# A decoder layer on one core: five places for probabilities in cross attention, outputs taken a pair later, VectorE's side work spread; experts with one table of results and adding scatters

## The chip, the cores and the metric

The kernel runs on one core of a Trainium2 chip. The metric is the device time of one launch in microseconds (us), as the median of several runs. The core has five engines with queues of their own: TensorE (PE) multiplies matrices into PSUM, VectorE (DVE) and ScalarE (ACT) work on PSUM and SBUF, GpSimd (POOL) works on SBUF, and SyncE (SP) issues transfers (DMAs). They meet only at semaphores. PEld is TensorE's loading of weights.

## The reference: what is computed

One decoder layer with post-normalisation, in f32, over 8 batches of 512 rows of 256. Three stages follow each other, each adding to its input and normalising the sum:

- self attention (16 heads of 64, across the batch of 8, for each of the 512 positions);
- cross attention of the 512 rows of each batch with 1024 context rows: both are normalised with a gain and bias, keys are rotated with cos and sin, the scores are clipped to -11 and 11 before the softmax, and the heads' outputs go through Wo;
- a mixture of 8 experts (hidden size 512, SiLU gate) with the best 2 for each of 4096 tokens, plus one shared expert for all.

```
attn = jnp.clip(jnp.einsum('bhnd,bhsd->bhns', q, k) * scale, -11.0, 11.0)
out = jnp.einsum('bhns,bhsd->bhnd', jax.nn.softmax(attn, axis=-1), v) @ Wo + bo
...
h = jnp.einsum('bsd,edh->bseh', x, W1) * jax.nn.silu(jnp.einsum('bsd,edh->bseh', x, W3))
out = sum over the two experts of (h @ W2) * w + shared expert
x = layernorm(x + out)
```

Products that need more than the matmul's own precision are made in three terms, from a high part (an f32r copy by ScalarE) and a low part (what the copy left out, a subtraction on VectorE or GpSimd).

## The kernel before

**Cross attention** (`cross_attention`) loops over 8 batches. A batch has two halves (g) of 8 heads; a half first makes keys and values in 8 tiles (`keys_values`, L881; the keys are rotated on VectorE and turned by TensorE, L917), and then goes through 4 pairs (p) of heads. A pair has 4 steps (j) of two units (a); a unit is 128 context rows by 2 heads by 512 queries, so 128x1024 values.

The work of one unit passes five engines' queues: TensorE makes the scores (L837, L845) into one of two pairs of PSUM banks; ScalarE takes the exponential into SBUF (L1071); GpSimd clips it there (L816, the clip of the scores done on their exponentials); TensorE multiplies the clipped unit with the values (L958); VectorE adds it to the pair's running sum `acc` (L1218, L1221). The exponentials have four places in `probs`, two for each parity of the step (`at_step`), so one of step j waits for `pv_done` and `acc_ready` of step j-2.

TensorE's order is written out: scores of the next step, in step 0 also the sums of the last pair (L865, a matmul of `acc` with ones) and the queries of the next (L857), then the products with the values. In the second half a step of each pair also transposes context rows for the next batch (L890).

What each pair leaves is worked up during the next: `inverse` takes the reciprocal of the sums in four quarters (L1194), `o_scaled` multiplies (L1201) into the single tile `o`, `o_hi` copies its high part on ScalarE (L1005), and `o_lo` the low one on VectorE (L1205); the project with Wo (L972) comes at the half's end. All of this stands in VectorE's queue between the accumulations, with the low part of the next queries (`q_lo`, L1173), and for the next batch the statistics of its rows (L1101, first half), their normalising (L1112) and the low part of the turned context (`context_lo`, L1116; second half). ScalarE has `o_hi` of pair p-1 at the end of step 3 of pair p, ahead of pair p+1's first exponentials. GpSimd has one power of a small tile for that normalising (L820), behind the second half's first two clips.

**Experts** (`experts`): 4096 tokens go in 16 dense units of 256 through the shared expert, and then sorted by expert in 39 units. Routing makes a place for each token and expert; 64 indirect DMAs scatter the rows into the sorted table `xs`. For each unit TensorE runs `first` (W3, W1; L1664) and `second` (W2; L1682), and between the halves of `first` it turns the rows of the next unit (`turn`, L1645). SP loads rows (`load_rows`, L1475) and weights (`load_w`, L1462) in one queue, in order; ScalarE and GpSimd and VectorE split the weights into high and low parts. GpSimd splits the next set's weights and then sends a unit's results (`send`, L1559): two indirect DMAs of 128 rows to the table `ys` in DRAM.

A token's two results go to two halves of `ys` (`SECOND` apart), so that no row is written twice; `goals` works out which. The dense results stay in SBUF (`take`, L1890) and eight additions join them with the input (`add_dense`, L1906), one in each of eight units from the third expert unit on. At the end both halves of `ys` are loaded in chunks of 512 tokens (L1504, L1771), GpSimd adds the two (`both`, L1574), VectorE adds the sum to the rest and takes the statistics (`combine`), GpSimd takes the power (`root`), ScalarE normalises (L1775), and SP stores.

## Time and profile before

| what | us |
|---|---|
| median of 3 runs (lowest, highest) | 3220.79 (3215.07, 3221.74) |
| profiled execution | 3219.01 |
| its span, first to last instruction | 3217.3 |
| mean granted TensorE clock | 0.965 |
| busy: PE, PEld | 2890.4 (90%), 1966.5 (61%) |
| busy: DVE, ACT, POOL | 2210.6 (69%), 1433.4 (45%), 1470.0 (46%) |

Cross attention lies from about 660 to 2610 us of the span and the experts from there to the end. Batch 3 (the fourth) of cross attention, from which most rows below are, goes from 1404.5 to 1642.5. A window's granted clock is a share of full speed: 1.00 is 2.4 GHz, and a stretch at 0.50 is 1.2 GHz. In the timelines a line is a run of like instructions: start, duration, engine, line, operation, output and inputs, count, and in brackets how long the engine was idle before it and what ended that.

### The profile page before, as it was taken

How to read it: one execution, taken by the hardware profiler on the slowest of the kernel's cores; microseconds unless marked ns; L12 is line 12 of the kernel's file. 1: busy time of each engine (PE TensorE's matmuls, PEld its weight loads, DVE VectorE, ACT ScalarE, POOL GpSimd, SP SyncE). 2: the span in 40 equal slices, each digit the busy share in tenths (PEclk: the TensorE clock that was granted, in tenths of full speed). 3: DMA queues.
4: the chain of work that ended last, by engine and by line, in shares of the span. 5: the costliest groups of instructions: out<-in, count | busy, mean ns of one | idle time of the engine just before them, and what ended most of it. 6: DMA issues, size and time to landing. Idle time of an engine off the chain costs nothing. (4 is left out here: it accounts for less than half of the span.)

```text
span 3217.3 us, 52631 instructions
## 1 busy us (share of the span) xinstructions
PE 2890.4 (90%) x17208; PEld 1966.5 (61%) x17256; DVE 2210.6 (69%) x3538; ACT 1433.4 (45%) x2076; POOL 1470.0 (46%) x1060
## 2 busy tenths in 40 slices
PE   6999999969999999999999999999899879999993
PEld 4888888844554454454454454454454449999992
DVE  3555555557768777678767777767767774598886
ACT  2222222253554553554554554554554532455553
POOL 1222222225445545545545545545545525466666
PEclk9999999989999999999999999999999989999996
DMA  9000000020010010010010010010010023266665
GB/s 255 14 15 14 15 14 15 14 66 8 14 39 10 14 41 7 14 41 7 14 41 7 14 41 7 14 41 7 14 41 7 14 79 117 101 210 222 225 223 192
DMA packets 137039, 180.91 MB, mean 56 GB/s; under 512 B 16992, under 2 KB 96864, under 8 KB 136736
## 3 DMA queue, kind: packets, MB, share of 16 engines
q1 hardware_dynamic: 115696, 143.74, 14.7%
q10 hardware_dynamic: 14224, 14.58, 1.7%
q0 software_dynamic: 6816, 18.75, 1.7%
q8 instruction: 166, 2.72, 0.4%
q14 instruction: 137, 1.12, 0.1%
HBM read 118.54 MB, written 41.71 MB: 50 GB/s over the span
## 5 line engine op out<-in xcount | busy, mean ns | idle before, releaser
L816 POOL TENSOR_SCALAR raw<-raw 128x1024 f32<-128x1024 f32 x512 | 737.7, 1441 | 452.8 <-ACT raw L1071 431.6
L1071 ACT ACTIVATE raw<-b_ps 128x1024 f32<-128x1024 f32 x512 | 498.7, 1020 | 398.3 <-PE b_ps L845 299.0
L1221 DVE TENSOR_TENSOR b_acc<-b_acc,raw 128x1024 f32<-128x1024 f32 x384 | 507.9, 1323 | 133.9 <-POOL raw L816 118.5
L958 PE MATMUL b_ps<-raw 128*64 128x512 f32 x2048 | 513.5, 617 | 43.4 <-POOL raw L816 43.0
L837 PE MATMUL b_ps<-b_QQ,b_KT 128*128 128x512 f32 x1024 | 334.9, 437 | 96.9 <-ACT raw L1071 92.6
L837 PEld LDWEIGHTS b_ps<-b_QQ,b_KT 128*128 128x128 f32 x1024 | 168.4, 191 | 336.4 <-ACT raw L1071 191.7
L802 POOL TENSOR_TENSOR b_QQ<-raw,b_QQ 128x512 fp32r<-128x512 f32 x128 | 165.5, 1293 | 390.6 <-ACT b_QQ L1025 390.6
L1664 PE MATMUL c_ps<-c_xT_l,c_w_h 128*128 128x256 f32 x1504 | 306.0, 287 | 8.6 <-DVE c_xT_l L1934 4.2
L958 PEld LDWEIGHTS b_ps<-raw 128*64 128x64 f32 x2048 | 121.3, 138 | 314.2 <-POOL raw L816 160.0
L1664 PEld LDWEIGHTS c_ps<-c_xT_l,c_w_h 128*128 128x128 f32 x1504 | 243.3, 192 | 14.4 <-issue 14.0
L1194 DVE RECIPROCAL b_r<-b_ps 128x128 f32<-128x128 f32 x256 | 234.6, 937 | 15.2 <-PE b_ps L865 13.7
L1542 POOL TENSOR_TENSOR c_w_l<-c_raw,c_w_h 128x1024 fp32r<-128x1024 f32 x80 | 169.5, 2138 | 151.0 <-ACT c_w_h L1715 151.0
L273 POOL TENSOR_TENSOR a_Pe<-a_Sc,a_same 128x2048 f32<-128x2048 f32 x32 | 117.7, 3679 | 234.8 <-DVE a_Sc L517 161.6
L1218 DVE TENSOR_TENSOR b_acc<-raw 128x1024 f32<-128x1024 f32 x64 | 85.3, 1333 | 196.5 <-POOL raw L816 196.5
L845 PE MATMUL b_ps<-b_QQ,b_KT 64*128 64x512 f32 x1024 | 194.7, 459 | 0.0
L501 DVE TENSOR_REDUCE a_Sc<-a_ps 128x32 f32<-128x512 f32 x128 | 80.9, 684 | 149.8 <-PE a_ps L331 149.8
L1664 PE MATMUL c_ps<-c_xT_l,c_w_l 128*128 128x256 f32 x624 | 176.4, 283 | 0.0
L1738 ACT ACTIVATE c_hT_h<-c_hid 128x512 fp32r<-128x512 f32 x110 | 69.5, 632 | 209.3 <-DVE c_hid L1913 209.3
L1045 ACT ACTIVATE b_KT<-b_ps 128x512 fp32r<-128x512 f32 x256 | 138.7, 598 | 33.0 <-PE b_ps L917 33.0
L1124 DVE TENSOR_TENSOR raw<-b_ps,b_cos 128x512 f32<-128x512 f32 x129 | 88.8, 689 | 90.5 <-PE b_ps L881 85.7
L1005 ACT ACTIVATE b_OT_h<-b_o 128x512 fp32r<-128x512 f32 x64 | 40.4, 631 | 225.0 <-DVE b_o L1201 225.0
L1025 ACT ACTIVATE b_QQ<-raw 128x512 fp32r<-128x512 f32 x129 | 81.6, 632 | 130.2 <-DVE raw L1136 129.9
(261 smaller groups left out, 6784.4 us busy)
## 6 DMA issues: line engine op xcount, KB each, us to landing
c_raw<-in_L_ffn_W_dram SPq DMA_DIRECT2D x117, 512.0 KB, 4.4
b_QQ<-b_QQ SPq DMA_DIRECT2D x128, 128.0 KB, 2.4
xs<-zeros ACTq DMA_DIRECT2D x1, 10140.0 KB, 66.6
c_xg<-xs SPq DMA_DIRECT2D x39, 260.0 KB, 5.8
b_rows<-in_ctx_dram SPq DMA_DIRECT2D x9, 1024.0 KB, 7.4
a_xt<-in_x_dram SPq DMA_DIRECT2D x72, 64.0 KB, 2.2
b_rows<-x SPq DMA_DIRECT2D x9, 512.0 KB, 7.0
x<-a_x1t SPq DMA_DIRECT2D x64, 64.0 KB, 1.9
```

The costliest lines, as they stand in the source:

```text
L273: pool.tensor_tensor(Pe[:, :, :].rearrange("p h (t b) -> p (h t) b", b=BI), Sc[:, t % 2].rearrange("p h t -> p (h t)").unsqueeze(2).broadc ...
L802: pool.tensor_tensor(nat[:, :, 1:3, :], krot[:, t % 2, :].rearrange("p (q a n) -> p q a n", a=2, n=HD), nat[:, :, 0::3, :].bitcast(F32), A ...
L816: pool.tensor_scalar(pr, pr, HI, LO, ALU.min, ALU.max).then_inc(clipped, 1)
L837: pe.matmul(bank(key, hh), KT[:, 2 * p + hh, t * P:(t + 1) * P], QQ[:, n % 2, hh, 0, :], start=True, stop=False)
L845: mm = pe.matmul(bank(key, hh), KT[own, 2 * p + hh, t * P:(t + 1) * P], QQ[own, n % 2, hh, 1, :], start=False, stop=True)
L958: mm = pe.matmul(bank(key)[hh * HD:(hh + 1) * HD, :], V[:, t, (2 * p + hh) * HD:(2 * p + hh + 1) * HD], probs[:, at_step(j, a), hh * B:(hh ...
L1045: drain(key, act.activation(KT[:, 4 * a:4 * a + 4, t * P:(t + 1) * P], bank(key).rearrange("p (h n) -> p h n", n=P), ACT.Copy))
L1071: ins = act.activation(probs[:, at_step(j, a), :], both(key), ACT.Exp, scale=SCALE)
L1194: ins = dve.reciprocal(r[:, a * P:(a + 1) * P], bank(key)[:, a * P:(a + 1) * P])
L1221: dve.tensor_tensor(total, total, pr, ALU.add).then_inc(acc_ready, 1)
L1542: pool.tensor_tensor(WS[m][n % 2][1][:, cols], raw[:, n % 2, m, cols], WS[m][n % 2][0][:, cols].bitcast(F32), ALU.subtract).then_inc(w_rea ...
L1664: mm = pe.matmul(ps[:, 2 * s + m, (hb % 2) * T:(hb % 2 + 1) * T], lhsT, rhs, start=(a == 0), stop=(a == 3 * KD - 1))
```

## The change

Cross attention:
- The exponentials have five places, the four of `probs` and a tile `fifth`, taken in turn by units counted through the half. An exponential waits for `pv_done` and `acc_ready` of the unit five before it; `pv_done` counts units instead of steps. The query tile `QQ` is split into `QH` and a smaller `QL`, and `knat` lies over a part of `QH` and `fifth`.
- ScalarE takes `o_hi` of pair p-2 at step 2 of pair p (the last but one behind the loop).
- VectorE's side work is ordered anew: `inverse` has one quarter at (1,0), (2,0), (2,1) and (3,0) each, `o_lo` moves to (3,0), `o_scaled` to (3,1), the row statistics to (0,0), the normalising of four row tiles is cut into two and two, and `context_lo` goes to (1,0). GpSimd's power of the second half comes behind step 1's clips.

Experts:
- `ys` has one row for each token (and spare ones). The dense result is added to the input as it is taken out of PSUM, SP stores it into `ys` (`store_dense`), and each send adds to `ys` (`compute_op`). A send waits until the one before has landed, the first until all dense results have.
- Seven of the eight dense stores stand in SP's queue ahead of the first `load_rows`, the eighth behind the second.
- `add_dense`, `both` and the additions in `combine` go. At the end each chunk is loaded once, by SP and ScalarE in turn.

```diff
+        def unit(p, j, a):
+            return (p * 4 + j) * 2 + a
+        def place(u):
+            n = (u + 2) % 5
+            return probs[:, n, :] if n < 4 else fifth[:, :]
...
-                                if (g, p, j) == (1, 0, 0):
+                                if (g, p, j) == (1, 0, 1):
                                     pool.wait_ge(var_ready, 2 * b + 2)
                                     pool.tensor_tensor(rs[:, :], ve[:, :], mhalf[:, :], ALU.pow).then_inc(rstd_ready, 1)
...
-                                mm.then_inc(pv_done, 1)
+                                    mm.then_inc(pv_done, 1)
...
-                                    if (p, j) >= (0, 2):
-                                        before = step(g, p, j) - 2
-                                        act.wait_ge(pv_done, b * (8 * PG) + before + 1)
-                                        act.wait_ge(acc_ready, b * (16 * PG) + before * 2 + a + 1)
-                                    ins = act.activation(probs[:, at_step(j, a), :], both(key), ACT.Exp, scale=SCALE)
+                                    u = unit(p, j, a)
+                                    if u >= 5:
+                                        act.wait_ge(pv_done, b * (16 * PG) + g * (8 * PG) + u - 4)
+                                        act.wait_ge(acc_ready, b * (16 * PG) + g * (8 * PG) + u - 4)
+                                    ins = act.activation(place(unit(p, j, a)), both(key), ACT.Exp, scale=SCALE)
...
-                                if j == 3 and p:
-                                    o_hi(b, g, p - 1)
+                                if j == 2 and p >= 2:
+                                    o_hi(b, g, p - 2)
+                        o_hi(b, g, PG - 2)
...
-                                    if 0 < p < PG - 1 and at == (3, 0):
-                                        o_scaled(p - 1)
-                                    if p:
-                                        quarters = {(1, 0): (0,), (2, 0): (1,), (2, 1): (2, 3)}
-                                        if p == PG - 1:
-                                            quarters = {(1, 0): (0,), (1, 1): (1,), (2, 0): (2,), (2, 1): (3,)}
-                                        for quarter in quarters.get(at, ()):
-                                            inverse(p - 1, quarter)
                                     if p + 1 < PG and at == (1, 1):
                                         q_lo(p + 1)
-                                    if p >= 2 and at == (0, 0):
+                                    if p and at in ((1, 0), (2, 0), (2, 1), (3, 0)):
+                                        inverse(p - 1, ((1, 0), (2, 0), (2, 1), (3, 0)).index(at))
+                                    if p >= 2 and at == (3, 0):
                                         o_lo(p - 2)
+                                    if 0 < p < PG - 1 and at == (3, 1):
+                                        o_scaled(p - 1)
...
+                def store_dense(c):
+                    sp.wait_ge(y_drained, 2 * c + 2)
+                    sp.dma_start(totals(c), dense[c]).then_inc(totals_in, 16)
...
+                for c in range(CH - 1):
+                    store_dense(c)
                 sp.wait_ge(scattered, 16 * 2 * NT)
                 load_rows(0)
                 load_rows(1)
+                store_dense(CH - 1)
...
                 def send(j):
                     pool.wait_ge(y_drained, DENSE + j + 1)
+                    if j:
+                        pool.wait_ge(sent[(j - 1) % 2], 16 * TT * ((j - 1) // 2 + 1))
+                    else:
+                        pool.wait_ge(totals_in, 16 * CH)
                     for t in range(TT):
                         pool.indirect_dma_start(
...
-                            in_=yr[:, j % 2, t, :], in_offset=None).then_inc(sent[j % 2], 16)
+                            in_=yr[:, j % 2, t, :], in_offset=None, compute_op=ALU.add).then_inc(sent[j % 2], 16)
...
-                        ins = dve.tensor_copy(dense[u // 2][:, 2 * (u % 2):2 * (u % 2) + 2, :].rearrange("p t d -> p (t d)"), src)
+                        ins = dve.tensor_tensor(dense[u // 2][:, 2 * (u % 2):2 * (u % 2) + 2, :],
+                                                src.rearrange("p (t d) -> p t d", d=D),
+                                                y[:, 2 * u:2 * u + 2, 0:D], ALU.add)
...
-                    if DENSE + 2 <= u < DENSE + 2 + CH:
-                        add_dense(u - DENSE - 2)
...
-                    dve.wait_ge(pooled, c + 1)
-                    dve.wait_ge(dense_added, c + 1)
-                    at = y[:, c * CT:(c + 1) * CT, 0:D]
-                    chained(dve.tensor_tensor(at, at, dense[c], ALU.add))
+                    dve.wait_ge(x_in[c], 32)
```

## Rows read from the trace of the kernel before

**Rows 1.** TensorE's waits in batch 3: waiter, releaser, us, times, longest
```profile
PE b_ps L837 <- ACT raw L1071: 11.8, 13, 2.7
PE b_ps L958 <- POOL raw L816: 5.4, 6, 1.1
```

**Rows 2.** Windows at batch 3's sums: length; busy PE, PEld, DVE, ACT, POOL; clock
```profile
1433.20:1456.30 23.10, 22.20 (x104) 9.79 (x103) 15.35 (x15) 14.59 (x21) 18.51 (x13) 1.00 0.05 13
1456.30:1475.90 19.60, 17.64 (x76) 6.93 (x76) 15.59 (x18) 9.20 (x11) 12.78 (x9) 1.00 0.06 14
...
1495.50:1510.20 14.70, 12.27 (x54) 3.98 (x53) 13.17 (x15) 5.82 (x6) 9.74 (x7) 1.00 0.01 2
1545.00:1570.80 25.80, 23.12 (x110) 10.38 (x110) 16.01 (x29) 15.75 (x22) 17.61 (x13) 1.00 0.05 11
1570.80:1594.10 23.30, 19.05 (x80) 7.66 (x82) 18.73 (x21) 10.95 (x14) 11.84 (x9) 0.95 0.05 12
1594.10:1615.60 21.50, 18.78 (x80) 7.38 (x80) 16.89 (x21) 10.58 (x13) 10.56 (x8) 0.97 0.06 13
1615.60:1632.70 17.10, 14.79 (x59) 4.81 (x57) 12.72 (x13) 7.11 (x8) 8.67 (x6) 0.90 0.00 0
```

**Rows 3.** TensorE's timeline: pair 1 of the first half, pair 0 of the second
```profile
1456.30 1.08 PE L865 MATMUL b_ps<-b_acc,b_ones 128*64 128x512 f32 x4 [0.28 <-DVE b_acc L1221]
...
1458.89 1.94 PE L958 MATMUL b_ps<-raw 128*64 128x512 f32 x8
...
1469.93 1.94 PE L958 MATMUL b_ps<-raw 128*64 128x512 f32 x8
...
1566.19 0.66 PE L890 MATMUL b_ps<-ident,b_rows 128*128 128x128 f32 x4 [0.64 <-DVE b_rows L1112]
```

**Rows 4.** ScalarE's timeline at the end of pair 1 of the first half
```profile
1472.05 0.63 ACT L1005 ACTIVATE b_OT_h<-b_o 128x512 fp32r<-128x512 f32 x1 [3.81 <-DVE b_o L1201]
```

**Rows 5.** GpSimd's and VectorE's timelines, then two lines' durations in ns: min/median/max
```profile
1473.78 2.17 POOL L816 TENSOR_SCALAR raw<-raw 128x1024 f32<-128x1024 f32 x2 [3.44 <-ACT raw L1071]
...
1505.24 3.55 POOL L816 TENSOR_SCALAR raw<-raw 128x1024 f32<-128x1024 f32 x2 [0.77 <-ACT raw L1071]
...
1506.67 1.22 DVE L1221 TENSOR_TENSOR b_acc<-b_acc,raw 128x1024 f32<-128x1024 f32 x1
...
L1221 DVE TENSOR_TENSOR b_acc<-b_acc,raw x384: 1153/1225/2056, 722.5 to 2588.3; 128x1024 f32<-128x1024 f32 x192
...
L1112 DVE TENSOR_SCALAR b_rows<-b_rows,b_mv,b_rs x108: 395/406/1207, 672.9 to 2553.5; 128x256 f32<-128x256 f32 x108
```

**Rows 6.** Timelines of SP, VectorE, TensorE at the first expert units; loads' landing (us)
```profile
2765.16 0.82 SPq L1475 DMA_DIRECT2D c_xg<-xs  x2
...
2780.04 0.69 DVE L1890 COPY c_dense<-c_ps 128x512 f32<-128x512 f32 x1 [0.74 <-PE c_ps L1682]
...
2798.40 0.68 DVE L1890 COPY c_dense<-c_ps 128x512 f32<-128x512 f32 x1
...
2782.72 0.60 PE L1645 MATMUL c_ps<-ident,c_xg 128*128 128x128 f32 x4
...
2800.86 0.60 PE L1645 MATMUL c_ps<-ident,c_xg 128*128 128x128 f32 x4
...
c_xg<-xs SPq DMA_DIRECT2D x39, 260.0 KB, 5.8
```

**Rows 7.** Windows: an expert unit with `add_dense`, one without; columns as above
```profile
2817.30:2827.40 10.10, 10.10 (x87) 10.10 (x86) 9.19 (x20) 5.64 (x9) 6.74 (x4) 1.00 0.60 211
...
2907.40:2916.80 9.40, 9.27 (x78) 9.09 (x77) 8.07 (x18) 5.51 (x9) 6.08 (x4) 1.00 0.67 224
```

**Rows 8.** Scatters' landing (us); windows: last chunk's statistics, final loads to the end
```profile
c_ys<-c_yr,c_goal_u POOLq DMA_INDIRECT x78, 2.4
...
3206.50:3209.90 3.40, 0.00 (x0) 0.00 (x0) 3.25 (x12) 2.08 (x5) 2.06 (x2) 0.50 0.14 47
3167.90:3217.30 49.40, 0.00 (x0) 0.00 (x0) 32.91 (x88) 16.48 (x32) 33.77 (x16) 0.50 0.78 255
```

More of the change, by code:

```diff
@@ L812, in _ @@
                                 for a in range(2):
-                                    pr = probs[:, at_step(j, a), :]
+                                    pr = place(unit(p, j, a))
                                     wait_drained(pool, ("s", g, p, j, a), b)
@@ L959, in _ @@
                                                        V[:, t, (2 * p + hh) * HD:(2 * p + hh + 1) * HD],
-                                                       probs[:, at_step(j, a), hh * B:(hh + 1) * B],
+                                                       place(unit(p, j, a))[:, hh * B:(hh + 1) * B],
                                                        start=(t == 0), stop=(t == CT - 1))
-                                mm.then_inc(pv_done, 1)
+                                    mm.then_inc(pv_done, 1)
                         def project(a, pairs):
@@ L999, in q_hi @@
                         own = slice(hh * HD, (hh + 1) * HD)
-                        ins = act.activation(QQ[own, n % 2, hh, 0, :], bank(key)[own, :], ACT.Copy)
+                        ins = act.activation(QH[own, n % 2, hh, :], bank(key)[own, :], ACT.Copy)
                     ins.then_inc(qh_ready, 1)
@@ L1172, in q_lo @@
                                 own = slice(hh * HD, (hh + 1) * HD)
-                                ins = dve.tensor_tensor(QQ[own, n % 2, hh, 1, :], bank(key)[own, :],
-                                                        QQ[own, n % 2, hh, 0, :].bitcast(F32), ALU.subtract)
+                                ins = dve.tensor_tensor(QL[own, n % 2, :], bank(key)[own, :],
+                                                        QH[own, n % 2, hh, :].bitcast(F32), ALU.subtract)
                             ins.then_inc(q_ready, 1)
@@ L1212, in _ @@
                                     at = (j, a)
-                                    pr = probs[:, at_step(j, a), :]
+                                    pr = place(unit(p, j, a))
                                     total = acc[:, p % 2].rearrange("p h n -> p (h n)")
@@ L1217, in _ @@
                                     if at == (0, 1):
-                                        dve.tensor_tensor(total, probs[:, at_step(0, 0), :], pr, ALU.add).then_inc(acc_ready, 2)
+                                        dve.tensor_tensor(total, place(unit(p, 0, 0)), pr, ALU.add).then_inc(acc_ready, 2)
                                     elif j:
@@ L1242, in _ @@
                                         variances(b, FIRST + b * TAKEN + ROWS)
-                                    if g == 1 and p < 3 and at == (((2, 0), (0, 1), (0, 1))[p]):
-                                        if p == 0:
-                                            dve.wait_ge(rstd_ready, 2 * b + 2)
-                                        for t in range(4 * p, 4 * p + 4):
-                                            normalise(t, rows[:, t, :], rows[:, t, :], normed)
-                                    if g == 1 and p and at == (0, 1):
+                                    if g == 1 and p < 3:
+                                        halves = ((2, 0), (2, 1)) if p == 0 else ((0, 0), (0, 1))
+                                        if at in halves:
+                                            if (p, at) == (0, (2, 0)):
+                                                dve.wait_ge(rstd_ready, 2 * b + 2)
+                                            t0 = 4 * p + 2 * halves.index(at)
+                                            for t in (t0, t0 + 1):
+                                                normalise(t, rows[:, t, :], rows[:, t, :], normed)
+                                    if g == 1 and p and at == (1, 0):
                                         context_lo(p - 1)
@@ L1337, in experts @@
         dense = [over("dense", c, 0) for c in range(CH)]
-        other = [raw[:, 0, c, :].rearrange("p (t d) -> p t d", d=D) if c < 2 else over("other", c, 1) for c in range(CH)]
         wr = sb("c_wr", [P, KD, E])
@@ L1447, in logit_bank, with totals @@
             return ps[:, 7 - 2 * (c % 2), (c // 2) * CT * E:(c // 2 + 1) * CT * E]
-        def results(half, c):
-            return ys[half * SECOND + 1 + c * 512:half * SECOND + 1 + (c + 1) * 512].rearrange("(t p) d -> p t d", p=P)
+        def totals(c):
+            return ys[1 + c * 512:1 + (c + 1) * 512].rearrange("(t p) d -> p t d", p=P)
         with nc.Block() as block:
@@ L1501, in _ @@
                     sp.wait_ge(sent[k], 16 * TT * ((TILES + 1 - k) // 2))
-                for c in range(CH):
-                    sp.wait_ge(dense_added, c + 1)
-                    sp.dma_start(dense[c], results(0, c)).then_inc(x_in[c], 16)
+                for c in range(0, CH, 2):
+                    sp.dma_start(y[:, c * CT:(c + 1) * CT, 0:D], totals(c)).then_inc(x_in[c], 16)
                 for c in range(CH):
@@ L1570, in _ @@
                 send(TILES - 1)
-                def both(c):
-                    pool.wait_ge(x_in[c], 48)
-                    pool.tensor_tensor(dense[c], dense[c], other[c], ALU.add).then_inc(pooled, 1)
                 def root(c):
@@ L1582, in _ @@
                 for c in range(CH):
-                    both(c)
-                    if c:
-                        root(c - 1)
-                root(CH - 1)
+                    root(c)
             @block.tensor
@@ L1767, in _ @@
                     act.wait_ge(sent[k], 16 * TT * ((TILES + 1 - k) // 2))
-                for m in range(2):
-                    wait_split(act, SETS - 1, m)
-                for c in range(CH):
-                    act.dma_start(other[c], results(1, c)).then_inc(x_in[c], 16)
+                for c in range(1, CH, 2):
+                    act.dma_start(y[:, c * CT:(c + 1) * CT, 0:D], totals(c)).then_inc(x_in[c], 16)
                 for c in range(CH):
@@ L1899, in take @@
                     ins.then_inc(y_drained, 1)
-                def add_dense(c):
-                    dve.wait_ge(scattered, 16 * 2 * NT)
-                    dve.wait_ge(y_drained, 2 * c + 2)
-                    at = y[:, c * CT:(c + 1) * CT, 0:D]
-                    dve.tensor_tensor(at, at, dense[c], ALU.add).then_inc(dense_added, 1)
                 def product(u, s):
```

43 lines of the change are left out of this document (18 added, 25 removed).

## The prediction

> **What bounds the kernel now.** I read the busy table first, then the waits of TensorE over one batch of cross attention, then windows cut at the pairs, and last each engine's timeline around a pair's end. The chain that ended last reaches back only through the experts, so it says nothing of the 1950 us of cross attention. There TensorE waits in one batch 11.8 us for exponentials and 5.4 us for clipped probabilities [rows 1]. The windows show where: the same pair of heads takes 19.6 us in a first half but 23.3 and 21.5 us in a second, and the four of a first half end with one of 14.7 us [rows 2]. Without a gap a pair with queries needs 2.59 us for sums and queries and four steps of (1469.93 - 1458.89) / 3 = 3.68 us, together 17.3 us [rows 3]. What is above that is one stall at the pair's end: ScalarE stands 3.81 us before the o_hi copy, waiting for o_scaled on VectorE, with the next pair's exponentials queued behind it [rows 4].
>
> There is a second limit close by. A clip on GpSimd takes 1.08 us when VectorE is quiet (2.17 for two), but two clips took 3.55 us when an accumulation ran at 1506.67: the first ended when that began, the second started when it had ended; the two operations' shortest are 1.15 us for the accumulation and 0.40 for a normalise of one row tile [rows 5]. So clips and accumulations go one after the other. Eight clips and seven accumulations are 8 x 1.08 + 7 x 1.15 = 16.7 us of a pair.
>
> The Trainium skill, page "SBUF — State Buffer", section "SBUF: two separate sides", calls the port pair of VectorE and GpSimd an exclusive lock held for a whole instruction, by a VectorE operation with two SBUF inputs too. By it clips and accumulations add up as I add them; were the port shared in proportion, TensorE alone would set the pairs, which is rival A.
>
> **The change part by part.** The sums are made against the profiled execution (3219.0 us, span 3217.3), which is 1.8 us under the median of the runs.
>
> *Output copies a pair later, five places, spread side work.* The o_hi copy of pair p-2 stands at step 2 of pair p, where o_scaled is a pair old, so ScalarE no longer waits 3.81 us. An exponential waits for the unit five back, not for a whole step two back; that slack is about one unit, 1.8 us of TensorE. It costs no instruction. What is late next is the port, pair by pair:
> - First half, pair 1: TensorE 17.3, port 16.7; both near full, so I add 0.4: 17.7 against 19.6, gain 1.9. Pair 2 has an o_lo on the port as well (half the accumulation's size, about 0.6): gain 1.8. Pair 3 was at the port already (six clips and seven accumulations are 14.5 of its 14.7 us) and now gets an o_lo that stood in its first unit: loss 0.4. Pair 0 stays. Sum 3.3.
> - Second half, pair 0: 25.8 against 23.1 in the first half, of which the four added transposes are 0.6 [rows 2, 3]. The power on GpSimd goes behind the second unit's clips: of the 2.1 left I take 1.5. Below nothing it is bounded by the later normalise, two rows after (2,1): about 1.2 lost if the transposes wait for it. Pair 1: port 16.7 + four normalises of 0.41 [rows 5] + context_lo 0.6 = 18.9, with 0.5 of imperfect packing 19.4 against 23.3: 3.9. Pair 2, with o_lo, 20.0 against 21.5: 1.5. Pair 3: loss 0.3. Sum 6.6.
> - Clock: a last pair at granted clock 0.90 took 17.1 us, the first half's 14.7 at 1.00; 0.6 of the difference is transposes, 1.8 is clock [rows 2]. In this batch three pairs of the second half have a reduced clock, each behind such a stall [rows 2]; with shorter ones I take back two thirds of that loss a batch, 1.2.
>
> Per batch 3.3 + 6.6 + 1.2 = 11.1, for eight batches 89 us. The bounds: nothing gained in pairs 1 and 2 of the second half and half elsewhere, 4 a batch (32 us); TensorE alone as limit, 14.5 a batch (116 us), with all clock back 20 (160 us). The 14.5 are the two waits' 17.2 [rows 1] less 2.7 that I leave at the half's ends and behind the context's high part.
>
> *pv_done by unit, QL/QH split:* the same matmuls and copies, operands elsewhere; the place of five overlaps the key tile whose transposes ScalarE has read before unit 2. Nothing.
>
> *Experts, dense results.* The copy out of PSUM becomes an addition of the same size, 0.69 us either way (nothing). Eight additions on VectorE go: their units take 10.1 us, later ones 9.4 [rows 7]: 8 x 0.7 = 5.6 gained. One small operation of the goals goes, off TensorE's path: nothing.
>
> *The stores in SP's queue.* Seven stores now stand ahead of the first row loads, which were issued at 2765.16. The seventh waits for the dense result of unit 13, taken at 2780.04 + 0.69 = 2780.7. Two issues are 0.8 and the load lands 5.8 after its issue: 2787.4, where the transposes wanted it at 2782.72: 4.7 us of idle TensorE [rows 6]. The eighth store waits for unit 15, taken at 2798.40 + 0.68 + 4.7 = 2803.8; behind it queue the weight loads of set 3 and the next rows (four issues, 1.7, then 5.8): 2811.3, where the transposes at 2800.86 + 4.7 = 2805.6 wanted them: 5.7. Later sets are asked for early enough. With 2.5 us of reduced clock after each (the last pair above lost 1.8 so) this costs 15.5; bounds 5 (loads landing at half that) and 28 (the weights' second wave late too).
>
> *Adding scatters.* A plain scatter lands in 2.4 us, a load of rows in 5.8 [rows 6, 8]. No row shows an adding one: between 2.4 and 5.8 + 2.4 = 8.2. I take 4, since it is the same 128 rows on the same queue as the 2.4. Each send now waits for the one before; that was issued a unit (9.4 us) earlier, so GpSimd, whose next weight split is queued behind, waits for nothing. At the end the last two sends follow closely: 2 x (4 - 2.4) + 0.4 = 3.6 lost (0.4 to 12).
>
> The Trainium skill, page "DMA: Bandwidth & Descriptors", section "Rules for kernel authors", says an accumulating DMA reads its destination and writes it later. By it the add costs the read as well; with a row load's time for the read the end would lose 12 instead of 3.6, and the sum come to 3133.
>
> *The end.* From the loads' issue to the end are 49.4 us, paced by a sum on GpSimd and one on VectorE for each of eight chunks. Now 5.8 for the first load, eight chunks of VectorE's 3.25 - 1.2 (the sum of that size) plus waits = 2.2 each, and about 6 of the 7.4 us from the last statistic (3209.9) to the end [rows 8]: 29.4. Gain 20, less 3.6.
>
> Experts together: 5.6 + 20 - 3.6 - 15.5 = 6.5.
>
> **Sum:** 3219.0 - 89 - 6.5 = 3123.5, with the median's 1.8 about 3125 us; its own range is 3100 to 3150.
>
> **The rivals.**
> A. The port packs better than I add (GpSimd and VectorE merely slow each other) and TensorE bounds the pairs: 14.5 to 20 a batch, 27 to 71 us more than the forecast: 3098 to 3054, say 3090. For it: TensorE's waits on these two engines are 17.2 a batch [rows 1]. Against: the 3.55 us.
> B. The stall moves. VectorE is busy 18.73 us of the second half's pair 1 [rows 2], against the 17.3 + 0.6 that TensorE needs; its lag shows up at the sums and at the fifth place, and half is gained: 5 a batch, 40 in all, with the experts' 6.5: 3221 - 46 = 3175. Against it: pairs 0 and 3 give VectorE time to catch up.
> C. The adding scatter is slow. A send takes X us from its first issue to its last landing, and the next waits for that; above the unit's 9.4 us it holds GpSimd, behind it the next set's weight split, and so TensorE, 37 times. With 8.2 for a landing and about 1 for the second issue X is 9.2: nothing in the units and 8 at the end, 3133. It decides against the change from X = 11.7: 37 x 2.3 = 85 and 12 at the end. At 13 it is 133 + 15: about 3273. Against it: the 2.4 us of the plain scatter.
> D. It doesn't do what it says: exponentials still end on the same accumulation, and cross attention keeps its time: 3214.
>
> **How the numbers follow.** Forecast 0.58, A 0.18, B 0.14, C from 11.7 up 0.05 (below that it is within the forecast's range), D 0.05. The range 3075 to 3175 leaves out half of A, some of B, C and D. A difference within 0.2% (6.4 us) can't be told from none; D is half in it. Faster 0.92, same 0.03, slower 0.05.
>
> **What would show it.** Right: no o_hi wait on ScalarE in a pair; first-half pairs 1 and 2 at 17.5 to 18, second-half ones at 19 to 20.5; clips lengthened by accumulations and TensorE's remaining gaps ending on a clip; two idle stretches of about 5 us at the first experts' units; units of 9.4 throughout; some 30 us after the last scatter. Wrong: pairs still over 21 in second halves (B), below 18.2 (A), expert units above 9.6 (C).

## The result, and the profile after

Beside the kernel before on the same chip (3220.11 us median of 4 runs), the changed kernel took 3127.37 us (4 runs, 3115.70 to 3130.13): ratio 0.971, 95% interval 0.968 to 0.974. A second set of runs gave 3120.69 against 3225.01, 0.969 (0.966 to 0.973). The forecast was 3125 us, its own range 3100 to 3150 and that with the rivals 3075 to 3175; the measured time lies in both, 2 us from the forecast.

The profiled execution (3130.13 us, span 3128.4) splits as follows, beside a second profiled execution of the same kernel (span 3110.5, below called the repeat). Cross attention runs from its first scores to the experts' first matmul, the units from the first expert tile's transposes to the last's:

| us | before | after | repeat |
|---|---|---|---|
| up to cross attention | 711.1 | 708.3 | 711.8 |
| cross attention | 1902.7 | 1817.6 | 1802.9 |
| dense part of the experts | 169.0 | 172.1 | 170.2 |
| 38 expert units | 359.9 | 368.4 | 364.6 |
| from there to the end | 74.6 | 62.0 | 61.0 |

So cross attention gave nearly all of it: 85 us in this profile, 100 in the repeat. The experts gave 1 us in this one (603.5 to 602.5) and 8 in the repeat.

The windows of a batch at the sums (length; busy PE, PEld, DVE, ACT, POOL; granted clock; DMA), four pairs of the first half, then four of the second, here of batch 2:

```profile
1162.10:1185.10 23.00, 22.11 (x105) 10.01 (x104) 16.30 (x16) 14.70 (x21) 18.69 (x13) 1.00 0.05 13
1185.10:1202.90 17.80, 17.37 (x74) 6.90 (x74) 15.76 (x20) 8.63 (x10) 14.44 (x9) 1.00 0.07 16
1202.90:1220.80 17.90, 17.47 (x76) 6.91 (x74) 15.06 (x16) 9.46 (x11) 13.55 (x9) 1.00 0.06 15
1220.80:1236.70 15.90, 13.30 (x54) 3.90 (x52) 13.83 (x17) 6.34 (x7) 12.80 (x7) 0.95 0.01 2
1272.40:1298.90 26.50, 23.03 (x111) 10.33 (x109) 17.82 (x32) 15.80 (x22) 19.67 (x13) 1.00 0.05 11
1298.90:1317.20 18.30, 18.12 (x80) 7.23 (x78) 17.16 (x19) 10.32 (x12) 13.29 (x8) 1.00 0.07 16
1317.20:1335.40 18.20, 18.03 (x80) 7.42 (x78) 17.86 (x19) 10.77 (x13) 9.59 (x8) 1.00 0.07 15
1335.40:1351.20 15.80, 13.17 (x58) 4.45 (x57) 13.40 (x15) 7.69 (x9) 10.70 (x7) 1.00 0.00 0
```

Against [rows 2] pairs 1 and 2 fell from 19.6 to 17.9 in the first half and from 23.3 and 21.5 to 18.3 and 18.2 in the second. In all four TensorE's busy time is now within 0.5 us of the window. Pair 0 of the second half went the other way, from 25.8 to 26.5.

TensorE's waits over that batch (waiter, releaser, us, times, longest), and ScalarE at the place of [rows 4], in batch 3:

```profile
PE b_ps L967 <- POOL raw L825: 7.2, 9, 1.1
...
PE b_ps L846 <- ACT raw L1080: 1.1, 6, 0.2
...
PE b_ps L899 <- DVE b_rows L1122: 0.9, 1, 0.9
```

```profile
1441.34 0.63 ACT L1014 ACTIVATE b_OT_h<-b_o 128x512 fp32r<-128x512 f32 x1
```

The wait for exponentials went from 11.8 us a batch [rows 1] to 1.1 (and 0.2 for those in the fifth place), and the o_hi copy waits for nothing there (the next, behind the half's last exponential, still waits 6.12 us for o_scaled). What grew is the wait for clips, 5.4 to 7.2. The timelines of GpSimd, TensorE and VectorE at the end of a first half show where it sits:

```profile
1458.77 6.39 POOL L825 TENSOR_SCALAR raw<-raw 128x1024 f32<-128x1024 f32 x3
...
1460.90 1.08 PE L967 MATMUL b_ps<-raw 128*64 128x512 f32 x4 [0.44 <-POOL raw L825]
...
1463.04 1.23 DVE L1231 TENSOR_TENSOR b_acc<-b_acc,raw 128x1024 f32<-128x1024 f32 x1
...
1463.06 1.08 PE L967 MATMUL b_ps<-raw 128*64 128x512 f32 x4 [1.08 <-POOL raw L825]
...
1465.22 1.08 PE L967 MATMUL b_ps<-raw 128*64 128x512 f32 x4 [1.08 <-POOL raw L825]
...
1466.99 1.68 PE L874 MATMUL b_ps<-b_acc,b_ones 128*64 128x512 f32 x4 [0.69 <-DVE b_acc L1231]
```

Three clips take 6.39 us, 2.13 each, where one alone takes 1.08 [rows 5]; an accumulation of 1.2 us stands between one and the next. With no other work left TensorE follows at that pitch.

In the experts, the landing of the scatters (median us), GpSimd's waits over the units, and some links of the chain of waits:

```profile
c_ys<-c_yr,c_goal_u POOLq DMA_INDIRECT x78, 4.5
```

```profile
POOL c_ys L1574 <- DMA c_ys<-c_yr,c_goal_u: 59.9, 29, 3.7
```

```profile
2799.59 1.56 POOL c_ys L1574
...
2801.46 8.83 DMA c_ys<-c_yr,c_goal_u
...
2811.02 1.56 POOL c_ys L1574
...
2812.89 6.92 DMA c_ys<-c_yr,c_goal_u
...
2820.55 1.58 POOL c_ys L1574
```

A send's first issue follows that of the send before by 9.5 to 11.4 us here: the first issue, 1.87 with what follows it, then 6.9 to 8.8 from the start of the second issue to its landing, then the next send. But for the second and third, which the second stall below and a reduced clock behind it lengthen to 14.7 and 11.4 us, the units of TensorE are 9.06 to 9.13 us up to the fifteenth; from the next on, at 9.2 to 11.5, the sends set them, as a run below tests. TensorE's first two late tiles, answering [rows 6], and the window from the final loads to the end, answering [rows 8]:

```profile
2697.96 0.66 PE L1653 MATMUL c_ps<-ident,c_xg 128*128 128x128 f32 x4 [2.30 <-DMA c_xg<-xs]
...
2721.82 1.11 PE L1653 MATMUL c_ps<-ident,c_xg 128*128 128x128 f32 x4 [5.51 <-DMA c_xg<-xs]
```

```profile
3099.57:3128.40 28.83, 0.00 (x0) 0.00 (x0) 15.64 (x80) 16.06 (x32) 8.10 (x8) 0.50 0.87 291
```

### The profile page after: what moved, and what is told of

It reads as the page before. It is cut to its first block and busy times, and to the rows that moved or that the text cites. A ratio compares the mean times of both kernels' runs of the same rounds, so it can differ in the third digit from the quotient of the medians.

```text
span 3128.4 us, 52086 instructions
## 1 busy us (share of the span) xinstructions
PE 2871.6 (92%) x17208; PEld 1966.8 (63%) x17256; DVE 2198.0 (70%) x3444; ACT 1435.1 (46%) x2076; POOL 1581.4 (51%) x1051
## 5 line engine op out<-in xcount | busy, mean ns | idle before, releaser
L1080 ACT ACTIVATE raw<-b_ps 128x1024 f32<-128x1024 f32 x416 | 410.7, 1021 | 366.6 <-PE b_ps L854 318.6
L967 PE MATMUL b_ps<-raw 128*64 128x512 f32 x1664 | 423.7, 612 | 57.2 <-POOL raw L825 57.2
L1231 DVE TENSOR_TENSOR b_acc<-b_acc,raw 128x1024 f32<-128x1024 f32 x304 | 399.3, 1313 | 89.9 <-POOL raw L825 80.3
L811 POOL TENSOR_TENSOR b_knat<-raw,b_knat 128x512 fp32r<-128x512 f32 x128 | 165.4, 1292 | 404.2 <-ACT b_knat L1034 404.2
L846 PE MATMUL b_ps<-b_QH,b_KT 128*128 128x512 f32 x1024 | 325.2, 430 | 14.8 <-ACT raw L1080 9.1
L846 PEld LDWEIGHTS b_ps<-b_QH,b_KT 128*128 128x128 f32 x1024 | 168.8, 189 | 245.1 <-issue 157.4
L854 PE MATMUL b_ps<-b_QL,b_KT 64*128 64x512 f32 x1024 | 188.1, 445 | 0.0
L825 POOL TENSOR_SCALAR b_fifth<-b_fifth 128x1024 f32<-128x1024 f32 x96 | 137.1, 1428 | 81.3 <-ACT b_fifth L1080 76.8
L1574 POOL DMA_INDIRECT c_ys<-c_yr,c_goal_u x78 | 127.8, 1639 | 75.2 <-DMA c_ys<-c_yr,c_goal_u 59.9
L1820 DVE TENSOR_TENSOR c_w_l<-c_raw,c_w_h 128x1024 fp32r<-128x1024 f32 (+1 forms) x80 | 128.6, 1607 | 22.9 <-ACT c_w_h L1723 22.9
```

What stands on the lines that cost most here:

```text
L811: pool.tensor_tensor(nat[:, :, 1:3, :], krot[:, t % 2, :].rearrange("p (q a n) -> p q a n", a=2, n=HD), nat[:, :, 0::3, :].bitcast(F32), A ...
L825: pool.tensor_scalar(pr, pr, HI, LO, ALU.min, ALU.max).then_inc(clipped, 1)
L846: pe.matmul(bank(key, hh), KT[:, 2 * p + hh, t * P:(t + 1) * P], QH[:, n % 2, hh, :], start=True, stop=False)
L854: mm = pe.matmul(bank(key, hh), KT[own, 2 * p + hh, t * P:(t + 1) * P], QL[own, n % 2, :], start=False, stop=True)
L967: mm = pe.matmul(bank(key)[hh * HD:(hh + 1) * HD, :], V[:, t, (2 * p + hh) * HD:(2 * p + hh + 1) * HD], place(unit(p, j, a))[:, hh * B:(hh ...
L1080: ins = act.activation(place(unit(p, j, a)), both(key), ACT.Exp, scale=SCALE)
```

## The experiments

**Each half of the change alone.** Two kernels: the changed cross attention with the experts of before, and the reverse.

> The changed cross attention with the experts of before. Theory (the parts add up: in the two profiles cross attention gives 85 us and the experts 1): 3135 us (3130 to 3140), with the first expert units at 9.4 to 10.1 us as before. Rival (the experts pay or gain by what cross attention leaves, a clock or a filled queue): outside 3130 to 3140.

> The changed experts with the cross attention of before. Theory (what the end gives, 20 us, and the units and stalls cost, 19 us, nearly cancel): 3219 us, no difference from before within 0.2%. Rival (the gain that the prediction worked out, 6.5 us, is there and the profiles hid it): 3213 us or less.

Cross attention alone: 3117.70 us against 3224.25, ratio 0.967 (0.965 to 0.969), outside the expected band on the fast side. Experts alone: 3220.36, ratio 0.998 (0.9965 to 1.000), as the theory had it; their parts are 172.4, 369.9 and 61.3, together 603.6 us against 603.5. So the experts' edits cancel, within an interval that reaches down to 3213 us, and the gain is cross attention's. Its size was misjudged from one profile: here cross attention took 1803.4 us, 14 less than in the profile after, though the pairs have the same lengths but for three. The next run says why.

**The changed kernel again.** No edit.

> The changed kernel itself, once more, beside the three below. Of four profiles with its cross attention that part took 1818, 1803, 1802 and 1808 us with 69, 30, 26 and 42 us of it at half clock. Theory (the pairs are always the same, the reduced clock is not, and the first profile had much of it): 1800 to 1818 us for cross attention with no pair changed, 3110 to 3130 in all. Rival (the experts' part of the change slows cross attention): 1815 us or more for cross attention, 3125 us or more.

3120.69 us (0.969, 0.966 to 0.973). The windows over all of cross attention, after and repeat (columns as above):

```profile
708.30:2525.80 1817.50, 1702.26 (x8112) 919.54 (x8110) 1413.98 (x1802) 934.47 (x1284) 1036.93 (x674) 0.98 0.08 21
```

```profile
711.80:2514.70 1802.90, 1685.85 (x8112) 910.32 (x8111) 1416.77 (x1802) 934.18 (x1284) 1037.23 (x674) 0.99 0.08 21
```

The repeat's pairs agree with those of the profile after to 0.03 us, but for three second-half pairs 0 that had a reduced clock there (27.3 instead of 26.5). Most of the rest of the difference lies between the halves, from a half's last sums to the next half's first scores: 39.7 us (to the next batch) and 35.7 (within a batch) on average after, 39.1 and 34.9 in the repeat. Summed over cross attention, TensorE had 110 us at half clock before, 69 after and 30 in the repeat. The theory holds: the profile after was a long one by its clock. The pairs, 166.2 us a batch before (both halves) and 153.4 in the repeat, give 12.8 us a batch.

**Four places instead of five.**

```
-            n = (u + 2) % 5
+            n = (u + 2) % 4
...
-                                    if u >= 5:
-                                        act.wait_ge(pv_done, ... + u - 4)
-                                        act.wait_ge(acc_ready, ... + u - 4)
+                                    if u >= 4:
+                                        act.wait_ge(pv_done, ... + u - 3)
+                                        act.wait_ge(acc_ready, ... + u - 3)
```

> The changed kernel with four places for probabilities, so that an exponential waits for the unit four back. Theory (the later output copies took the stall away; four units of TensorE are some 8.9 us, which is longer than one exponential, clip and accumulation after another): pairs 1 and 2 at most 0.5 us longer, 3125 to 3135 us. Rival (the fifth place is what lets the exponentials run on): pairs 1 and 2 at 19.5 to 21.5 us, 3155 us or more.

3122.65 us, ratio 0.967 (0.964 to 0.969). Pair 1 of a first and of a second half:

```profile
1647.50:1665.40 17.90, 17.47 (x76) 6.91 (x76) 15.82 (x20) 8.62 (x11) 14.54 (x9) 1.00 0.07 16
...
1760.40:1778.70 18.30, 18.13 (x80) 7.23 (x78) 17.16 (x19) 10.33 (x12) 13.29 (x8) 1.00 0.07 16
```

No pair is longer. With the outputs taken later, the fifth place buys nothing that can be measured. The time is a little under the expected band.

**Outputs where they were.** Five places and the spread side work stay.

```
-                                if j == 2 and p >= 2:
-                                    o_hi(b, g, p - 2)
-                        o_hi(b, g, PG - 2)
+                                if j == 3 and p:
+                                    o_hi(b, g, p - 1)
```

On VectorE o_scaled, inverse and o_lo stand at the units of before as well.

> The changed kernel with the outputs taken where they were before: the scaling behind unit (3,0) of the next pair, the high copy at that pair's end, the low copy in the first unit of the pair after it. The five places and the spread side work stay. Theory (the stall of ScalarE at the high copy, 3.8 us, is back, less about one unit of 1.8 us that the fifth place gives): pairs 1 and 2 at 19 to 20.5 us, 3155 to 3185 us in all. Rival (five places alone were enough): pairs within 0.5 us of the changed kernel, 3125 to 3135 us.

3193.51 us, ratio 0.991 (0.989 to 0.993), a little above the expected band. ScalarE at the end of a first half's pair 1, and the windows of pairs 1 and 2 of both halves:

```profile
1697.75 0.63 ACT L1014 ACTIVATE b_OT_h<-b_o 128x512 fp32r<-128x512 f32 x1 [3.81 <-DVE b_o L1210]
```

```profile
1682.10:1701.60 19.50, 17.54 (x76) 6.89 (x76) 16.44 (x21) 9.10 (x11) 12.77 (x9) 1.00 0.06 14
1701.60:1721.10 19.50, 17.54 (x76) 6.90 (x74) 15.60 (x18) 9.46 (x11) 11.04 (x9) 1.00 0.06 13
1797.00:1818.00 21.00, 18.22 (x82) 7.36 (x80) 17.87 (x21) 10.86 (x14) 11.37 (x8) 1.00 0.06 14
1818.00:1841.40 23.40, 20.70 (x82) 8.38 (x82) 17.36 (x19) 10.95 (x14) 11.20 (x8) 0.86 0.05 12
```

The stall is back with the same 3.81 us as in [rows 4], the first-half pairs are 19.5 us, nearly the 19.6 of before, and cross attention is 1884 us, 81 above the repeat. Five places did not take the stall away; taking the outputs later did. (Moving only some of an output's steps was not tried; the quarters of `inverse` went back with them.) These 81 us are not all of the 100: cross attention is still some 18 us under that of before here (1902.7), most of it in the pairs, 164.3 us a batch against 166.2. So the five places, the side work or both give that much where the outputs are early. Beside late outputs each of the two can go without loss, the one in the run above, the other in the run below; taking away both at once was not tried.

**Side work where it was.** Statistics and normalises unsplit behind unit (0,1), the power behind (0,0).

```
-                                if (g, p, j) == (1, 0, 1):
+                                if (g, p, j) == (1, 0, 0):
...
-                                        halves = ((2, 0), (2, 1)) if p == 0 else ((0, 0), (0, 1))
+                                    if g == 1 and p < 3 and at == (((2, 0), (0, 1), (0, 1))[p]):
```

> The changed kernel with VectorE's side work where it was before: statistics and the context's normalises in one piece behind unit (0,1), the context's low part there too, and the power on GpSimd behind unit (0,0). Theory (it is the later power and the two halves of normalises that made pair 0 of the second half longer, 26.5 us against 25.8; in the other pairs the same work stands at the same port): pair 0 of the second half 25 to 26, pair 1 at 18.3 to 19, 3120 to 3130 us. Rival (the spreading is part of the gain): second halves 2 us longer or more, 3145 us or more.

3122.20 us, ratio 0.967 (0.966 to 0.969). Pair 0 of a first half, pairs 0 and 1 of a second:

```profile
1622.20:1645.90 23.70, 22.20 (x105) 9.99 (x104) 15.95 (x15) 14.70 (x21) 19.46 (x13) 1.00 0.05 12
...
1731.80:1757.50 25.70, 23.05 (x109) 10.33 (x107) 16.08 (x29) 15.81 (x22) 17.63 (x13) 1.00 0.05 11
1757.50:1775.90 18.40, 18.13 (x80) 7.35 (x79) 17.09 (x19) 10.31 (x12) 13.45 (x9) 1.00 0.07 16
```

The 0.7 us of the second half's pair 0 come back (25.7), the first half's pair 0 loses as much (23.7 against 23.0), and the pairs 3 cancel: the first half's is 0.5 shorter, the second's 0.5 longer. Pairs 1 and 2 don't care where four normalises stand. Over a batch it is 153.4 us either way: beside late outputs, spreading the statistics, the normalises and `context_lo` and moving the power gave nothing.

**Clips of half the size.** One line: `half = pr[:, 0:B]` is clipped instead of `pr`.

> The changed kernel with clips of half the size; left out is the clipping of every second head's probabilities. A clip falls from 1.08 us to some 0.6 and the work of the port that GpSimd and VectorE share by 4 us a pair. Theory (since the change TensorE sets pairs 1 and 2, the port only the end of a half): pairs 1 and 2 lose no more than their one gap of 0.43 us (17.4 to 17.9 in first halves, 17.9 to 18.3 in second), pair 3 falls by 1 us or more, 3080 to 3105 us. Rival (the port still sets the pairs): pairs 1 and 2 fall by 0.8 us or more.

3061.09 us, ratio 0.950 (0.947 to 0.953). Pairs 1 and 3 of a first half, then 0, 1, 2 of a second:

```profile
1617.80:1635.10 17.30, 17.30 (x78) 7.14 (x77) 14.12 (x18) 8.96 (x11) 7.45 (x8) 1.00 0.07 16
...
1652.30:1666.50 14.20, 12.26 (x56) 4.11 (x55) 13.17 (x17) 6.33 (x7) 7.42 (x6) 1.00 0.01 2
1701.20:1725.30 24.10, 23.05 (x111) 10.33 (x109) 16.06 (x32) 15.68 (x23) 14.47 (x13) 1.00 0.05 12
1725.30:1743.60 18.30, 18.06 (x82) 7.39 (x80) 15.76 (x20) 10.31 (x12) 7.46 (x8) 1.00 0.07 16
1743.60:1761.80 18.20, 18.03 (x80) 7.40 (x78) 16.01 (x19) 10.76 (x13) 6.93 (x8) 1.00 0.07 15
```

In second halves GpSimd's busy time falls from 13.3 and 9.6 us to 7.5 and 6.9, and the pairs 1 and 2 stay at 18.3 and 18.2: there TensorE sets them, and the port (what VectorE and GpSimd share) does not. In first halves they lose 0.66 us, between the two expectations, a part of the clips' pace that TensorE still waited for. Where GpSimd or the port does bind is pair 0 of the second half (26.5 to 24.1) and the ends of the halves (15.9 to 14.2, and 15.7 to 15.0). This run can't tell the two apart, since a half clip is also shorter in itself; the last run, which takes an accumulation of VectorE's out there, can.

**Scatters that write instead of adding.** One argument: `compute_op=ALU.add` goes.

> The changed kernel with scatters that write instead of adding; left out is the addition of the two experts' results and of the dense result. Theory (an adding scatter takes so long from its issue to its landing that the next one waits on GpSimd, the weight split behind it comes late, and so TensorE): the units after the sixteenth fall from 9.2 to 11.5 us to about 9.06 throughout, 16 us in all, a landing is 2.4 to 3 us, the last two sends are about 4 us shorter: 3107 us (3102 to 3112). Rival (those units are long because the weight loads or the rows arrive late, whatever the scatter does): units as before this edit, only the last sends shorter: 3123 us.

3094.53 us, ratio 0.961 (0.959 to 0.962), below the expected band: cross attention took 1801.9 us in its profile, 16 less than in the profile after. Its experts are 580.2 us against 602.5. Landings, and GpSimd's instructions over the units (count, busy us, mean ns, idle before), first of the plain kernel, then of the one after:

```profile
c_ys<-c_yr,c_goal_u POOLq DMA_INDIRECT x78, 2.4
...
L1574 POOL DMA_INDIRECT c_ys<-c_yr,c_goal_u x50 | 48.8, 975 | 11.5 <-issue 11.4
```

```profile
L1574 POOL DMA_INDIRECT c_ys<-c_yr,c_goal_u x54 | 86.4, 1600 | 57.2 <-DMA c_ys<-c_yr,c_goal_u 48.0 <-issue 9.2
```

Behind the two stalls the units are 9.06 us up to the 28th and at most 9.23 then, 353.0 in all, 15.4 less; from there to the end it is 54.9 instead of 62.0. The theory holds: adding costs 22.5 us against the profile after (15.4 and 7.1), 17.7 against the repeat (11.6 and 6.1).

**The goals' two small operations back, on top of the plain scatters.**

```
+                    dve.scalar_tensor_tensor(goal[:, 0, :], eid, own, nought[:, :], ALU.not_equal, ALU.mult)
...
-                    dve.tensor_tensor(goal_u[:, q, :], token, goal[:, 1, :], ALU.add)
+                    link(dve.tensor_tensor(goal[:, 3, :], goal[:, 0, :], token, ALU.add))
+                    dve.tensor_tensor(goal_u[:, q, :], goal[:, 3, :], goal[:, 1, :], ALU.add)
```

> The kernel with writing scatters of above (left out is the addition of the results) with the two small operations back that the change took out of VectorE's goals, one of them ahead of a wait of the chain. Its units took 9.06 us, those of the kernel before 9.45. Theory (these operations made VectorE's unit longer than TensorE's): the units are 9.35 to 9.5 us again, 353 us for the 38 units become 364 to 368. Rival (the units of before were longer by something else, the two tables or the plain scatters' traffic): 9.06 to 9.15.

One run, 3102.37 us. A unit without them and one with them:

```profile
2873.50:2882.60 9.10, 9.10 (x79) 9.10 (x78) 7.77 (x16) 5.44 (x9) 6.07 (x4) 1.00 0.70 226
```

```profile
2884.60:2894.00 9.40, 9.23 (x78) 9.06 (x77) 8.07 (x18) 5.56 (x8) 6.07 (x4) 1.00 0.72 224
```

The units are 9.45 us again, as before the change, though only from the 16th on (the 15th is 9.38): 361.9 us against 353.0. Two operations of 0.2 us were worth 0.39 us a unit. By which path is not shown: in such units VectorE is busy 8.1 us and waits 1.1 for ScalarE, never for TensorE, which would fit a loop of VectorE's that is the longer one.

**The last two dense stores later.**

```
-                for c in range(CH - 1):
+                for c in range(CH - 2):
                     store_dense(c)
...
                 load_rows(1)
-                store_dense(CH - 1)
+                store_dense(CH - 2)
...
                     load_w(n, 1, of_expert(W3, e))
+                    if n == 4:
+                        store_dense(CH - 1)
                     load_rows(n - 1)
```

> The changed kernel with the last two dense stores behind other issues of the sync engine's queue: the seventh behind the first two row loads, the eighth behind the second weight load of set 4. Theory (the rows of the first tiles come late because the stores stand ahead of them): the two idle stretches of TensorE at the first expert units, 2.3 and 5.5 us, go, and with them some clock: 3119 us (3116 to 3122). Rival (the loads are late by themselves, or what is gained is given back because GpSimd's sends bound the units behind): 3125 to 3128 us, with the stretches gone or not.

3111.01 us, ratio 0.964 (0.962 to 0.966). The first seven units are 9.06 us without a stall, but the sends bind from the eighth on, GpSimd waiting for them 75 us instead of 60:

```profile
POOL c_ys L1576 <- DMA c_ys<-c_yr,c_goal_u: 75.1, 36, 3.8
```

The units come to 366.4 us against 368.4 and, in the repeat, 364.6. The rival's mechanism is what the trace shows, its time is not what was measured: cross attention differs by 5 to 15 us of clock between these runs, so what the edit saved can't be read from the times. Nor from the units: in the seven profiles with the changed experts as they are they took 364.0 to 378.2 us.

**A better version.** On top of the moved stores, in each half's last pair the last unit but one is summed by TensorE.

```
+                for hh in range(2 if last else 0):
+                    pe.matmul(bank(key)[hh * HD:(hh + 1) * HD, :], ones[:, :],
+                              place(unit(p, 3, 0))[:, hh * B:(hh + 1) * B], start=True, stop=False)
                 pe.wait_ge(acc_ready, b * (16 * PG) + (step(g, p, 3) + 1) * 2)
...
+                                    elif (p, at) == (PG - 1, (3, 0)):
+                                        dve.wait_ge(acc_ready, b * (16 * PG) + n)
+                                        dve.sem_inc(acc_ready, 1)
```

> The changed kernel with the two dense stores moved as above, and in each half's last pair the sums of the last but one unit taken by TensorE straight from the probabilities, so that VectorE has one accumulation less there. Theory (the end of a half waits for clips that wait for accumulations, 1.08 us each; one less of them pulls the last clip ahead by 1.1 us, and the two matmuls more cost TensorE at most that gap): 0.5 to 0.8 us a half, 8 to 13 us in all under the version with the stores moved, about 3100 us. Rival (the added matmuls of 1.08 us take what the clip gives): within 3 us of that version, 3108 to 3114 us.

3086.05 us, ratio 0.958 (0.956 to 0.960): faster than both kernels. At the end of a half there is one gap of 1.08 us where there were two and one of 0.69:

```profile
1679.94 2.20 PE L971 MATMUL b_ps<-raw 128*64 128x512 f32 x8 [1.08 <-POOL raw L825]
...
1681.97 1.03 PE L874 MATMUL b_ps<-raw,b_ones 128*64 128x512 f32 x4
...
1682.83 1.03 PE L878 MATMUL b_ps<-b_acc,b_ones 128*64 128x512 f32 x4
```

Each pair 3 is 1.03 us shorter (15.90 to 14.87, 15.75 to 14.72), more than the 0.5 to 0.8 expected: 16.5 us over 16 halves. So the end of a half waits for VectorE's accumulations as well as for the clips. The rest of the difference lies where this edit changes nothing: the units took 356.4 us with the experts of the run before (366.4), GpSimd waiting 45 us for landings instead of 75.

## Why the prediction came out right

The total was right to 2 us. The first step, the stall at the high copy, was right; several terms behind it were mis-sized and cancelled, so that such closeness is in part luck.

- **The stall and its removal**: right. It is 3.81 us, it goes when the outputs are taken later and returns when they are not. The prediction shared the credit with the fifth place and the spreading; beside late outputs the runs give each of those two nothing, and with early outputs some 18 us to the two together.
- **What is late next**: half wrong. First-half pairs 1 and 2 were put at 17.7 and 17.8 and are 17.9 and 17.9. For second halves the port's sum (16.7 for clips and accumulations, 2.2 for normalises and context_lo, 0.5 of packing) gave 19.4 and 20.0; they are 18.3 and 18.2, TensorE's own time with the transposes. The gain in those two pairs was 8.6 us a batch, not 5.4. Rival A's limit holds in these two pairs; its total of 3090 does not, because the port does bind elsewhere. The sum added the normalises as if each took the port for its length. The trace does not show that: VectorE's and GpSimd's timelines at the start of a second half's pair 2 are

```profile
1318.43 2.34 DVE L1122 TENSOR_SCALAR b_rows<-b_rows,b_mv,b_rs 128x256 f32<-128x256 f32 x2
...
1318.45 2.18 POOL L825 TENSOR_SCALAR raw<-raw 128x1024 f32<-128x1024 f32 x2 [1.26 <-ACT raw L1080]
```

  Two clips beside two normalises take 2.18 us, where two alone take 2.17 [rows 5]; it is the normalises that wait, 2.34 us for what is 0.8 alone. All 37 clips of the profile after that met normalises and no other work of VectorE's have a median of 1.04 us and at most 1.17; the 59 that met none of its work have 1.04 to 1.05. Beside an accumulation a clip takes up to 2.08. Without the 1.6 us of normalises the port's sum is 17.3 us and with o_lo 17.9, under TensorE's 18.1 and 18.0. So rival A's better packing holds for the normalises, the forecast's adding up for the accumulations. Half clips and unsplit normalises both left 18.3 where it was.
- **Pair 0 of the second half**: wrong in sign. Forecast was a gain of 1.5; it lost 0.7. The power took 2.28 us of GpSimd before and held TensorE's products by 0.31 us; the later one stands 3.31 us there, beside VectorE's accumulation, and holds them by 0.89 (first the lines of before, then those of after):

```profile
1553.40 2.28 POOL L820 TENSOR_TENSOR b_rs<-b_ve,b_mhalf 128x12 f32<-128x12 f32 x1 [2.44 <-DVE b_ve L1109]
...
1556.86 1.08 PE L958 MATMUL b_ps<-raw 128*64 128x512 f32 x4 [0.31 <-POOL raw L816]
```

```profile
1284.04 3.31 POOL L829 TENSOR_TENSOR b_rs<-b_ve,b_mhalf 128x12 f32<-128x12 f32 x1
...
1288.54 1.08 PE L967 MATMUL b_ps<-raw 128*64 128x512 f32 x4 [0.89 <-POOL raw L825]
```

  The next products wait 1.08 us in both, and the transposes 0.9 us for a normalise instead of 0.64 [rows 3]; together that is about the 0.7. The run that put the power back unsplit the normalises too, so each one's share is as the traces read and was not tested alone.

- **Pairs 3**: losses of 0.4 and 0.3 were expected; against the means of before (15.7 and 16.3, some at a reduced clock) they are a loss of 0.2 and a gain of 0.6.
- **Clock**: 1.2 us a batch was an estimate from one batch, and no pair decides the clock. Time at half clock in cross attention went from 110 us to 69, or to 30 in the repeat. That alone moves the total by some 15 us.
- **One small goals operation: nothing.** Wrong. Two operations went, and they were worth 0.39 us a unit (9 us over the units when put back), though no single wait of TensorE showed it. That VectorE's unit was the longer one is argued, not shown.
- **Eight additions gone: 5.6.** Nearly right in size, by another count. The units of before were not 9.4 us throughout: seven took 9.06, then five (not eight) 10.1, then the rest 9.45. The run with the goals back has no additions; less the 7.9 us that its stalled units have over 9.07 its units are 354.0 us against 359.9.
- **SP's queue**: the two late loads are there, 2.30 and 5.51 us where 4.7 and 5.7 were worked out. A reduced clock follows the second alone: the granted clock is 0.51 for 5.2 us, and the unit is 2.3 us longer. So they cost some 10 us in this profile, not 15.5. What taking them away bought can't be told from the spread of the units (356 to 378 us), since the sends bind behind them.
- **Adding scatter**: landing assumed 4 us, measured 4.5 as the median of all, but 6.6 on average for the second scatter of a send, which the next send waits for, and up to 8.8; the issue, taken as unchanged, went from 0.96 to 1.60 us. So the send's cycle passed the unit's 9.06 us, which is rival C's mechanism at a small part of its price (some units are above its sign, 9.6): it needed no X of 11.7 to show, since the units had become shorter too. It cost 15.4 us in the units and 7.1 at the end (11.6 and 6.1 against the repeat), where 3.6 in all had been put.
- **The end**: 29.4 us from the loads on, measured 28.8. Right.

The Trainium skill, page "SBUF — State Buffer", section "SBUF: two separate sides", has a VectorE operation with two SBUF inputs and a GpSimd operation exclude each other for the whole instruction. At a half's end the trace agrees: 2.13 us from clip to clip, 1.08 of it the clip. In the middle of the pairs 1 and 2 of second halves this decides nothing, since TensorE is the longer one there.

## What to carry to other kernels

Ask of each instruction in an in-order queue how old its operand is: here outputs taken a pair later gave 81 of 100 us, and the extra buffer beside them none. When operations of two engines are added up as excluding each other, read for each kind of pair what the one does to the other's length: here an accumulation doubled a clip and a normalise left it as it was. The longest engine sets a pair, and what matters of the others is the places where that one has nothing else to do. A wait that a change adds between sends has to be held against the shortest cycle that the change itself makes possible, not against the old one.

## What the runs showed that was not expected

An indirect DMA that adds costs its issuer more, 1.60 us on GpSimd against 0.96 to 0.98 for one that writes, and lands in 4.5 us against 2.4, both medians of 78. The same experts' code took 364.0 to 378.2 us for its units in seven profiles; why is open. And nearly the same pairs came with cross attentions 15 us apart, most of it between the halves, with TensorE 39 us longer at half clock in the longer one.
